# Turning the gated rows of routed tiles through memory instead of on TensorE in a one-core mLSTM and mixture-of-experts kernel

## The chip, the cores and the metric

The kernel runs on one core of one Trainium2 chip. The time is device microseconds of one execution. Of the kernel before the change three executions were timed.

## The reference, cut to what matters

The input x has 8 x 512 = 4096 tokens of 1024 floats. The first half of the layer adds a gated mLSTM cross attention; the change does not touch it. The second half normalises the rows and adds a mixture of experts:

```
probs = softmax(flat @ router_w.T); topk_w, topk_idx = top_k(probs, 2)     # 16 experts, 2 for each token
shared = (silu(flat @ shared_gate_w) * (flat @ shared_up_w)) @ shared_down_w   # inner width 1024
xs = flat[sorted_tok]                                   # rows sorted by expert
g = ragged_dot(xs, gate_w, group_sizes); u = ragged_dot(xs, up_w, group_sizes) # inner width 512
dn = ragged_dot(silu(g) * u, down_w, group_sizes)
out = x + tanh(g_ffn) * (shared + scatter_add(sorted_w * dn))
```

Everything is float32. The product silu(g) * u, a tile of 128 tokens by 512, is what this text calls the gated rows, h. For the third matrix product h must stand with its 512 columns on the partitions, so each tile of h has to be turned.

## The kernel before, in words

The kernel has two blocks. The first, `mix_block`, does the attention, the routing and half of the shared expert. The second, `ffn_block`, runs the 16 routed experts over tiles of 128 gathered tokens (at least two tiles for an expert, 73 tiles in all) and after them the other half of the shared expert over 32 tiles. The change is in `ffn_block` alone. Each matrix product is made of three in a faster format: a high part of the one factor by a high part of the other, and the two mixed products with the low parts. So a tile takes 48 matmuls for gate and up (line 1608, into `p_g` and `p_up`) and 24 for down (line 1594, into `p_y`), and every operand, weights too, is split into a high part by ScalarE (a copy) and a low part by VectorE (a subtraction).

No planner sets the order. Each engine has a program of its own (`@block.sync`, `@block.gpsimd`, and so on), in which `tiles` (line 1172 and on) calls that engine's `body` once for each tile i; semaphores tie them together. PE is one tile ahead of itself: in the body of tile i it makes gate and up of tile i and then `down`, which is the third product of tile i-1. The turn of h of tile i-1 has to be done by then.

- Routed tiles before: `turn_h` of PE (line 1581) makes four transposes of 128x128 into the PSUM tile `p_h`, in the middle of gate and up of the next tile; ScalarE copies the high part out (`h_high`, line 1377), VectorE subtracts for the low part (`h_low`, line 1462), and `down` waits for that.
- Shared tiles, before and after: `h_store` (line 1366) sends h, 256 KB, from ScalarE's DMA queue to the memory tensor `mid_h`, in rows of 512 B. `h_quarters` (line 1372) waits until that has landed and fetches it back into h with four rows on one partition, 2 KB for each partition. VectorE's `turn_h` (line 1457) then turns squares of 32x32, ScalarE's `turned_high` (line 1383) takes the high part and `h_low` the low one.

ScalarE's body runs in this order: the weight split `split_gu` if the tile is its expert's first (8 pieces, line 1354), the right half of y out of PSUM (`y_right`, line 1406), the high part of the turned h, then a wait for gate and up, tanh (line 1422), the high part of the next x tile (`x_high`, line 1394), the left half of y (`y_left`, line 1401), and in a first tile `split_d` (4 pieces, line 1361). VectorE's body: low parts of the weights (line 1439) in a first tile, then h, then the turn of the next tile's x (`turn_x`, line 1473), then the two multiplications that make h (`silu_up`, lines 1485 and 1490), then the low part of x (`x_low`, line 1479), then in a first tile the low parts of the down weights.

SP's queue carries the weights (`load_weights`, line 1120) and the stores of y (`store_routed`, line 1223). The three weight tensors of an expert are 2 MB each; gate and up arrive in rows of 2 KB, down in rows of 16 KB. SP asks for those of expert e+1 after the last y store of expert e-1, when expert e's own are split, so in the second tile of expert e. GpSimd gathers the x rows of each routed tile (lines 1290 to 1300) through the third queue. In the page, q1 is SP's queue, q10 ScalarE's and q0 GpSimd's.

Of the kernel before, what the change touches and what calls it, by code (L numbers as in the profile page):

```python
# [15 lines left out]
NE, FE, FS = 16, 512, 1024  # L16
# [13 lines left out]
GUP = 8  # L30
# [1092 lines left out]
def ffn_block(nc, t, keep):  # L1123
# [4 lines left out]
    with ExitStack() as ctx:  # L1128
# [60 lines left out]
            body(n + (NCH - 1), n + (NCH - 2), NE, NCH - 1, False, "shared", True)  # L1189
            finish(n + NCH, n + (NCH - 1), NE, NCH)  # L1190

        def start(eng, e, less=0):

            return eng.value_load(starts_i[0:1, less, bass.ds(e, 1)], min_val=MIN_TILES - less, max_val=MAX_TILES - less)

        xn_quarters = t["xn"].rearrange("(c j t) (a d) -> c a j t d", t=4, j=32, a=4)
        xn_flat = t["xn"].rearrange("c (a d) -> (c a) d", a=4)
# [12 lines left out]

        @block.sync
        def _(sp):
            def load_weights(e):

                ge(sp, gu_split, GUP * e)
                weights_in(sp, stage, expert_weights(t, e, 1), slice(0, 2), (wg_in, wu_in))
                ge(sp, d_split, (PIECES - GUP) * e)
                weights_in(sp, stage, expert_weights(t, e, 1), slice(2, 3), (wd_in,))

            def store_routed(q):  # L1220

                sp.wait_ge(y_rdy, 2 * q + 2)
                sp.dma_start(t["y"][bass.ds(q * P, P), :], y[:, :]).then_inc(y_out, 16)

            def load_base(c):
                ge(sp, z_rdy, c)
                sp.dma_start(base_row[:, :], base_rows[c]).then_inc(base_in, 16)

            def store_joined(c):

                sp.wait_ge(z_rdy, c)
                sp.dma_start(z_rows[c - 1], y[:, :]).then_inc(z_out, 16)

            load_weights(1)

            store_routed(0)
            with sp.Fori(2, start(sp, 1)) as i:
                store_routed(i - 1)
            with sp.Fori(1, NE - 1) as e:
                store_routed(start(sp, e, 1))  # L1240
                load_weights(e + 1)
                with sp.Fori(start(sp, e) + 1, start(sp, e + 1)) as i:
                    store_routed(i - 1)
            store_routed(start(sp, NE - 1, 1))
            load_weights(NE)
            with sp.Fori(start(sp, NE - 1) + 1, start(sp, NE)) as i:
                store_routed(i - 1)
            store_routed(start(sp, NE, 1))
            before = start(sp, NE)

            def load_x(c):
                sp.wait_ge(x_turned, before + c)
                quarters_in(sp, c, xs_in)

            for n in range(2):
                sp.wait_ge(mid_out[n], 16 * NCH // 2)
            load_base(0)
            load_x(2)
            with sp.Fori(1, NCH - 4) as c:
                load_x(c + 2)  # L1260
                load_base(c)
                store_joined(c)
            for left in (4, 3, 2, 1):
                c = NCH - left
                if left > 2:
                    load_x(c + 2)
                if left > 1:
                    load_base(c)
                else:
                    ge(sp, gu_split, GUP * (NE + 1))  # L1270
                    sp.dma_start(last_base, base_rows[c]).then_inc(last_base_in, 16)
                store_joined(c)
            for n in range(2):
                half = slice(512 * n, 512 * n + 512)
                sp.wait_ge(last_z, n + 1)
                sp.dma_start(z_rows[NCH - 1][:, half], y[:, half]).then_inc(z_out, 16)
            sp.wait_ge(z_out, 16 * (NCH + 1))
# [67 lines left out]

        @block.scalar
        def _(act):
            def split_gu(i, e):

                act.wait_ge(wg_in, 16 * e + 16)  # L1350
                act.wait_ge(wu_in, 16 * e + 16)
                ge(act, gu_ps, i)
                for p in range(GUP):
                    nc.scalar.activation(w_hi[:, p, :], stage[:, p, :], ACT.Copy).then_inc(gu_hi, 1)

            def split_d(i, e, prev):
                act.wait_ge(wd_in, 16 * e + 16)
                if prev:
                    act.wait_ge(y_ps, 2 * i)
                for p in range(GUP, PIECES):  # L1360
                    nc.scalar.activation(w_hi[:, p, :], stage[:, p, :], ACT.Copy).then_inc(d_hi, 1)  # L1361

            def h_store(c):

                act.wait_ge(h_rdy, start(act, NE) + (c + 1))
                act.dma_start(t["h"].rearrange("a s f -> s a f"), h[:, :].rearrange("p (a f) -> p a f", a=4)
                              ).then_inc(hs_out, 16)

            def h_quarters(c):

                act.wait_ge(hs_out, 16 * c)
                act.dma_start(h[:, :], t["h"].rearrange("a (j t) f -> (a j) (t f)", t=4)).then_inc(hq_in, 16)

            def h_high(i):

                act.wait_ge(ht_ps, i)
                nc.scalar.activation(ht_hi[:, :, :], p_h[:, :, :], ACT.Copy).then_inc(ht_hi_rdy, 1)  # L1377

            def turned_high(c, q):

                act.wait_ge(y_ps, 2 * q)
                act.wait_ge(h_turned, c)
                nc.scalar.activation(ht_hi[:, :, :], h_t[:, :, :], ACT.Copy).then_inc(ht_hi_rdy, 1)

            def last_high(c):

                act.wait_ge(ht_ps, start(act, NE) + 1)
                nc.scalar.activation(ht_hi[:, :, :], p_h[:, :, :], ACT.Copy).then_inc(ht_hi_rdy, 1)

            def x_high(i):  # L1390

                act.wait_ge(x_turned, i + 1)
                for n in range(2):
                    nc.scalar.activation(xt_hi[:, 4 * n:4 * n + 4, :], x_t[:, 4 * n:4 * n + 4, :],  # L1394
                                         ACT.Copy).then_inc(xt_hi_rdy, 1)

            def y_left(q):

                ge(act, y_out, 16 * q)
                act.wait_ge(y_ps, 2 * q + 1)  # L1400
                nc.scalar.activation(y[:, 0:512], p_y[0][:, :], ACT.Copy).then_inc(y_rdy, 1)

            def y_right(q):

                act.wait_ge(y_ps, 2 * q)
                nc.scalar.activation(y[:, 512:D], p_y[1][:, :], ACT.Copy).then_inc(y_rdy, 1)

            def body(i, q, e, c, first, prev, last):
                if first and not (isinstance(i, int) and i == 0):
                    split_gu(i, e)  # L1410
                if callable(q):
                    q = q()

                if not (isinstance(i, int) and i < 2) and (c is None or isinstance(c, int) and c < 2):
                    y_right(q)
                if prev == "shared":
                    h_quarters(c)
                    turned_high(c, q)
                elif prev:
                    h_high(i)  # L1420
                act.wait_ge(gu_ps, i + 1)
                nc.scalar.activation(th[:, :], p_g[:, :], ACT.Tanh, scale=0.5).then_inc(tanh_rdy, 1)  # L1422
                if not last:
                    x_high(i + 1)
                    if c is not None:
                        h_store(c)
                if prev == "routed":
                    y_left(q)
                if first:
                    split_d(i, e, prev)  # L1430

            x_high(0)
            tiles(act, body, lambda i, q, e, c: last_high(c))

        @block.vector
        def _(dve):
# [13 lines left out]
                for p in range(GUP, PIECES):  # L1450
                    split(p, d_hi, (PIECES - GUP) * e + (p - GUP + 1), d_split)

            def turn_h(i, c):

                dve.wait_ge(xt_rdy, 2 * i)
                dve.wait_ge(hq_in, 16 * c)
                nc.vector.transpose(h_t[:, :, :].rearrange("p k (j t) -> p t k j", t=4),
                                    h[:, :].rearrange("p (t i k) -> p t k i", t=4, k=FE // P)).then_inc(h_turned, 1)

# [22 lines left out]
            def silu_up(i, c):  # L1482
# [2 lines left out]
                nc.vector.scalar_tensor_tensor(out=th[:, :], in0=th[:, :], scalar=1.0, in1=p_g[:, :],  # L1485
                                               op0=ALU.add, op1=ALU.mult).then_inc(silu_step, 1)
                dve.wait_ge(silu_step, i + 1)
                if c is not None:
                    ge(dve, h_turned, c)
                nc.vector.scalar_tensor_tensor(out=h[:, :], in0=th[:, :], scalar=0.5, in1=p_up[:, :],  # L1490
                                               op0=ALU.mult, op1=ALU.mult).then_inc(h_rdy, 1)

# [52 lines left out]
            def body(i, q, e, c, first, prev, last):  # L1545
                if first:
                    split_gu(i, e)
                if prev == "shared":
                    turn_h(i, c)
                    h_low(i, h_t)  # L1550
                elif prev:
                    h_low(i, p_h)
                if not last:
                    turn_x(i + 1, c)
                silu_up(i, c)
# [18 lines left out]
        def _(pe):  # L1574
# [23 lines left out]
            def body(i, q, e, c, first, prev, last):  # L1598
                ge(pe, h_rdy, i)
                for k in range(KD):  # L1600
# [3 lines left out]
                    for m, (a, w) in enumerate(trio):  # L1604
                        if m == 2:
                            pe.wait_ge(gu_split, GUP * e + (k + 1))
                        for out, o in ((p_g, 0), (p_up, FE)):
                            mm = nc.tensor.matmul(out[:, :], a[:, k, :], w[:, k, o:o + FE],  # L1608
                                                  start=(k == 0 and m == 0), stop=(k == KD - 1 and m == 2))
                    if k == 3 and prev == "routed":  # L1610
                        turn_h(i)
                mm.then_inc(gu_ps, 1)
                if prev:
                    down(i, e - 1 if first else e)
# [71 lines left out]
```

## Time and profile before

| what | value |
|---|---|
| median of three runs | 2929.71 us (2923.65 to 2931.17) |
| profiled execution, span | 2941.0 us |
| PE busy in it | 2784.3 us (95%) |
| VectorE busy | 1845.4 us (63%) |
| ScalarE busy | 1015.8 us (35%) |
| DMA, mean | 156 GB/s, 458.24 MB |
| routed tiles | about 1185 to 2421 us |
| shared tiles | about 2421 to 2941 us |

The profile comes from one execution. For it the page gives the span, from the first to the last instruction, and no other time of its own; the span is 11.3 us (0.4%) above the median of the timed runs. A matmul's busy time of about 0.39 us overlaps that of its neighbours, so the pace is read from the starts of successive groups, not from busy times. Times in the rows are microseconds from the span's start.

### The profile page before, as it was taken

The numbers are of one execution on the slowest core, as the hardware profiler recorded it, in microseconds if no ns is written. First come the engines' busy times: TensorE is split into PE (matmuls) and PEld (weight loads), VectorE is DVE, ScalarE is ACT, GpSimd is POOL, SyncE is SP. The second block draws the span as 40 slices with busy tenths as digits, with TensorE's granted clock in tenths as the row PEclk, the third lists the DMA queues.
The fourth block names the chain that finished last, engine by engine and source line by source line (L and its number), as shares of the span: only waits on it lengthen the run. The fifth ranks groups of instructions, "written<-read, shape, count | busy, mean of one in ns | idle before, by whom it ended". The sixth has DMA issues, their size and how long they took to land.

```text
span 2941.0 us, 49274 instructions
## 1 busy us (share of the span) xinstructions
PE 2784.3 (95%) x17322; PEld 2290.3 (78%) x17323; DVE 1845.4 (63%) x2800; ACT 1015.8 (35%) x1948; POOL 996.6 (34%) x1148
## 2 busy tenths in 40 slices
PE   3799999999999986999999999999999999999999
PEld 2677777777777774788888888888888888888887
DVE  3787878878887854454555545545545546767676
ACT  4445444444444421233333333333333331111111
POOL 1334433434344423343343443443443411111111
PEclk7799999999999997999999999999999999999999
DMA  6445545554555541344444444443443327666665
GB/s 196 148 158 170 159 141 162 166 153 152 162 169 159 145 166 65 136 150 150 145 150 148 146 153 144 146 153 143 148 152 143 100 108 213 182 203 183 203 182 182
DMA packets 243470, 458.24 MB, mean 156 GB/s; under 512 B 99696, under 2 KB 131824, under 8 KB 240624
## 3 DMA queue, kind: packets, MB, share of 16 engines
q1 hardware_dynamic: 116976, 333.62, 33.9%
q0 software_dynamic: 34880, 73.10, 8.1%
q10 hardware_dynamic: 91488, 49.82, 6.3%
q8 instruction: 81, 1.33, 0.2%
q14 instruction: 45, 0.37, 0.0%
HBM read 358.96 MB, written 115.31 MB: 161 GB/s over the span
## 4 chain that ended last, share of the span: by engine, by line
PE 59%; DVE 1%; issue 0%; ACT 0%; DMA 0%; SPq 0%; ACTq 0%; DVEq 0%
PE p_g_b L1608 19%; PE p_up_b L1608 19%; PE p_y_b L1594 19%; PE p_h_b L1581 1%; DVE x_t_b L1473 0%; DVE w_lo L1439 0%; DMA xn<-mid_xn 0%; ACT w_hi L1361 0%; SPq L1204 0%; DVE xt_lo_b L1479 0%; ACT xt_hi_b L1394 0%; DVE th_b L1485 0%; DVE x L1515 0%; DVE x L1506 0%; DVE y_b L1517 0%
## 5 line engine op out<-in xcount | busy, mean ns | idle before, releaser
L1300 POOL DMA_INDIRECT xn<-mid_xn,idx_q x284 | 304.5, 1072 | 512.6 <-DVE x_t_b L1473 424.6
L1608 PE MATMUL p_g_b<-w_hi,xt_hi_b 128*128 128x512 f32 x840 | 334.6, 398 | 19.8 <-DVE xt_lo_b L1479 16.9
L1594 PE MATMUL p_y_b<-w_hi,ht_hi_b 128*128 128x512 f32 x840 | 327.4, 390 | 1.9 <-DVE ht_lo_b L1462 1.9
L1608 PE MATMUL p_g_b<-w_lo,xt_hi_b 128*128 128x512 f32 x840 | 328.6, 391 | 0.0
L1608 PE MATMUL p_g_b<-w_hi,xt_lo_b 128*128 128x512 f32 x840 | 328.4, 391 | 0.0
L1608 PE MATMUL p_up_b<-w_hi,xt_lo_b 128*128 128x512 f32 x840 | 328.0, 390 | 0.0
L1608 PE MATMUL p_up_b<-w_hi,xt_hi_b 128*128 128x512 f32 x840 | 327.8, 390 | 0.0
L1608 PE MATMUL p_up_b<-w_lo,xt_hi_b 128*128 128x512 f32 x840 | 327.7, 390 | 0.0
L1594 PE MATMUL p_y_b<-w_hi,ht_lo_b 128*128 128x512 f32 x840 | 327.5, 390 | 0.0
L1594 PE MATMUL p_y_b<-w_lo,ht_hi_b 128*128 128x512 f32 x840 | 327.4, 390 | 0.0
L1462 DVE TENSOR_TENSOR ht_lo_b<-p_h_b,ht_hi_b 128x512 fp32r<-128x512 f32 x74 | 51.0, 690 | 367.5 <-ACT ht_hi_b L1377 367.5
L1439 DVE TENSOR_TENSOR w_lo<-stage,w_hi 128x1024 fp32r<-128x1024 f32 x200 | 230.2, 1219 | 79.8 <-ACT w_hi L1361 49.2
L1422 ACT ACTIVATE th_b<-p_g_b 128x512 f32<-128x512 f32 x105 | 62.8, 598 | 547.0 <-PE p_up_b L1608 543.6
L1485 DVE SCALAR_TENSOR_TENSOR th_b<-th_b,p_g_b 128x512 f32<-128x512 f32 x105 | 72.2, 688 | 281.0 <-ACT th_b L1422 271.9
L1473 DVE STREAM_TRANSPOSE x_t_b<-xn 128x1024 f32<-128x1024 f32 x104 | 235.0, 2259 | 16.6 <-PEq L76 12.6
L1006 PE MATMUL p_g<-w_hi,xt 128*128 128x512 f32 x512 | 212.8, 416 | 0.0
L1006 PE MATMUL p_up<-w_hi,xt 128*128 128x512 f32 x512 | 202.3, 395 | 0.0
L1608 PEld LDWEIGHTS p_g_b<-w_hi,xt_hi_b 128*128 128x128 f32 x840 | 158.9, 189 | 50.9 <-DVE xt_lo_b L1479 17.9
L1608 PEld LDWEIGHTS p_g_b<-w_lo,xt_hi_b 128*128 128x128 f32 x840 | 157.9, 188 | 38.9 <-DVE w_lo L1439 5.6
L1594 PEld LDWEIGHTS p_y_b<-w_hi,ht_hi_b 128*128 128x128 f32 x840 | 158.1, 188 | 34.9 <-DVE ht_lo_b L1462 2.1
L591 ACT ACTIVATE stage<-stage,cols 128x128 f32<-128x128 f32 x512 | 153.8, 389 | 90.4 <-POOL stage L456 90.3
L1608 PEld LDWEIGHTS p_g_b<-w_hi,xt_lo_b 128*128 128x128 f32 x840 | 157.9, 188 | 33.8
(224 smaller groups left out, 5585.8 us busy)
## 6 DMA issues: line engine op xcount, KB each, us to landing
mid_y<-y_b SPq DMA_DIRECT2D x73, 512.0 KB, 2.6
stage<-mid_g_row SPq DMA_DIRECT2D x64, 512.0 KB, 5.4
stage<-in_eg SPq DMA_DIRECT2D x16, 2048.0 KB
stage<-in_eu SPq DMA_DIRECT2D x16, 2048.0 KB
stage<-in_ed SPq DMA_DIRECT2D x16, 2048.0 KB
mid_y<-in_x SPq DMA_DIRECT2D x34, 512.0 KB
stage<-in_x SPq DMA_DIRECT2D x32, 512.0 KB
stage<-in_ctx_t ACTq DMA_DIRECT2D x32, 512.0 KB, 8.9
```

The costliest lines, as they stand in the source:

```text
L591: nc.scalar.activation(gbd[:, h, :], gbd[:, h, :], ACT.Exp, bias=cols[:, j, 0, h:h + 1]).then_inc(d_rdy, 1)
L1006: last = nc.tensor.matmul(out[:, :], xt[:, a, k, :], w[:, k, o:o + FE], start=(k == 0 and m == 0), stop=(k == KD - 1 and m == 2))
L1300: nc.gpsimd.indirect_dma_start(out=xg_parts[:, n, :], out_offset=None, in_=xn_flat, in_offset=bass.IndirectOffsetOnAxis(ap=idx_q[:, n:n + ...
L1422: nc.scalar.activation(th[:, :], p_g[:, :], ACT.Tanh, scale=0.5).then_inc(tanh_rdy, 1)
L1439: nc.vector.tensor_tensor(w_lo[:, p, :], stage[:, p, :], w_hi[:, p, :].bitcast(f32), ALU.subtract).then_inc(sem_lo, 1)
L1462: nc.vector.tensor_tensor(ht_lo[:, :, :], source[:, :, :], ht_hi[:, :, :].bitcast(f32), ALU.subtract).then_inc(ht_rdy, 1)
L1473: nc.vector.transpose(x_t[:, :, :].rearrange("p k (j t) -> p t k j", t=4), parts.rearrange("p t (i k) -> p t k i", k=KD)).then_inc(x_turne ...
L1485: nc.vector.scalar_tensor_tensor(out=th[:, :], in0=th[:, :], scalar=1.0, in1=p_g[:, :], op0=ALU.add, op1=ALU.mult).then_inc(silu_step, 1)
L1581: last = nc.tensor.transpose(p_h[:, k, :], h[:, k:FE:FE // P], ident[:, :])
L1594: last = nc.tensor.matmul(p_y[n][:, :], a[:, k, :], b[:, GUP + k, w], start=(k == 0 and m == 0), stop=(k == FE // P - 1 and m == 2))
L1608: mm = nc.tensor.matmul(out[:, :], a[:, k, :], w[:, k, o:o + FE], start=(k == 0 and m == 0), stop=(k == KD - 1 and m == 2))
```

## The change

Routed tiles take the way of the shared ones: PE's transposes go, and h of every tile is stored, fetched back and turned on VectorE. In an expert's first tile the fetch is issued in the middle of `split_gu`. `h_store` follows `x_high`; `silu_up` now waits in every tile until the turn of the tile before is done. PE's `turn_h` stays for the last tile alone, in `finish`. SP's `load_weights` is cut in two functions that are called one behind the other, and the loop of y stores is written out by one turn.

```diff
         def _(sp):
-            def load_weights(e):
+            def load_gate_up(e):
                 ge(sp, gu_split, GUP * e)
                 weights_in(sp, stage, expert_weights(t, e, 1), slice(0, 2), (wg_in, wu_in))
+            def load_down(e):
                 ge(sp, d_split, (PIECES - GUP) * e)
                 weights_in(sp, stage, expert_weights(t, e, 1), slice(2, 3), (wd_in,))
...
+            def store_expert(e, after):
+                store_routed(start(sp, e, 1))
+                load_gate_up(after)
+                load_down(after)
+                store_routed(start(sp, e, 0, MIN_TILES))
+                with sp.Fori(start(sp, e) + 2, start(sp, e + 1)) as i:
+                    store_routed(i - 1)
...
             with sp.Fori(1, NE - 1) as e:
-                store_routed(start(sp, e, 1))
-                load_weights(e + 1)
-                with sp.Fori(start(sp, e) + 1, start(sp, e + 1)) as i:
-                    store_routed(i - 1)
+                store_expert(e, e + 1)
...
         def _(act):
-            def split_gu(i, e):
+            def split_gu(i, e, prev):
...
                 for p in range(GUP):
+                    if p == GUP // 2 and prev:
+                        h_quarters(i)
                     nc.scalar.activation(w_hi[:, p, :], stage[:, p, :], ACT.Copy).then_inc(gu_hi, 1)
...
-                if prev == "shared":
-                    h_quarters(c)
-                    turned_high(c, q)
-                elif prev:
-                    h_high(i)
+                if prev:
+                    if not first:
+                        h_quarters(i)
+                    turned_high(i, q)
                 act.wait_ge(gu_ps, i + 1)
                 nc.scalar.activation(th[:, :], p_g[:, :], ACT.Tanh, scale=0.5).then_inc(tanh_rdy, 1)
                 if not last:
                     x_high(i + 1)
-                    if c is not None:
-                        h_store(c)
+                    h_store(i)
...
         def _(dve):
-                if prev == "shared":
-                    turn_h(i, c)
+                if prev:
+                    turn_h(i)
                     h_low(i, h_t)
-                elif prev:
-                    h_low(i, p_h)
...
-                if c is not None:
-                    ge(dve, h_turned, c)
+                ge(dve, h_turned, i)
...
         def _(pe):
-                    if k == 3 and prev == "routed":
-                        turn_h(i)
```

## Rows read from the trace of the kernel before

**Rows 1.** Page, busy time: us, share of the span, instructions.
```profile
PE 2784.3 (95%) x17322; PEld 2290.3 (78%) x17323; DVE 1845.4 (63%) x2800; ACT 1015.8 (35%) x1948; POOL 996.6 (34%) x1148
```
**Rows 2.** Page, DMA issues: count, KB each, median us to landing.
```profile
mid_y<-y_b SPq DMA_DIRECT2D x73, 512.0 KB, 2.6
stage<-in_eg SPq DMA_DIRECT2D x16, 2048.0 KB
```
**Rows 3.** Chain of waits, routed (1536 to 1571) and shared tiles: start, us, what.
```profile
1536.66 5.44 PE p_y_b L1594 x24
1547.54 0.47 PE p_h_b L1581 x4
1553.51 5.44 PE p_y_b L1594 x24
...
1570.59 5.44 PE p_y_b L1594 x24
...
2448.59 5.44 PE p_y_b L1594 x24
...
2464.91 5.44 PE p_y_b L1594 x24
```
**Rows 4.** Timeline, ScalarE and VectorE in one shared tile: start, us, engine, line.
```profile
2499.65 0.38 ACTq L1366 DMA_DIRECT2D mid_h<-h_b  x1
2502.68 0.33 ACTq L1372 DMA_DIRECT2D h_b<-mid_h  x1
...
2505.97 1.10 DVE L1457 STREAM_TRANSPOSE h_t_b<-h_b 128x512 f32<-128x512 f32 x1
...
2507.83 0.69 DVE L1462 TENSOR_TENSOR ht_lo_b<-h_t_b,ht_hi_b 128x512 fp32r<-128x512 f32 x1 [0.76 <-ACT ht_hi_b L1383]
```
**Rows 5.** One line's instructions, the fetch of h in shared tiles: time to landing.
```profile
DMA to landing us min/median/max: 2.6/2.6/2.7
```
**Rows 6.** Timeline, ScalarE and VectorE, first and second tile of one expert.
```profile
1557.42 7.70 ACT L1354 ACTIVATE w_hi<-stage 128x1024 fp32r<-128x1024 f32 x8 [0.56 <-issue]
...
1579.88 0.57 ACT L1406 ACTIVATE y_b<-p_y_b 128x512 f32<-128x512 f32 x1
...
1558.51 9.17 DVE L1439 TENSOR_TENSOR w_lo<-stage,w_hi 128x1024 fp32r<-128x1024 f32 x8 [1.72 <-ACT w_hi L1354]
...
1583.22 2.29 DVE L1473 STREAM_TRANSPOSE x_t_b<-xn 128x1024 f32<-128x1024 f32 x1
...
1588.82 0.69 DVE L1490 SCALAR_TENSOR_TENSOR h_b<-th_b,p_up_b 128x512 f32<-128x512 f32 x1
```
**Rows 7.** Timeline, SP's queue, same expert.
```profile
1582.77 3.23 SPq L1120 DMA_DIRECT2D stage<-in_ed  x1
1593.69 0.35 SPq L1223 DMA_DIRECT2D mid_y<-y_b  x1
```
**Rows 8.** DMA queues, 1585 to 1586: packets, MB, share of 16 engines.
```profile
q1 hardware_dynamic: 202, 0.41, 106.4%
```
**Rows 9.** DMA queues, 1598 to 1599.
```profile
q1 hardware_dynamic: 24, 0.39, 92.8%
q0 software_dynamic: 24, 0.00, 1.4%
```
**Rows 10.** One line's instructions, y store of 1593.69: time to landing.
```profile
DMA to landing us min/median/max: 9.1/9.1/9.1
```
**Rows 11.** One line's instructions, index loads of 1591.5 to 1593.1: time to landing.
```profile
DMA to landing us min/median/max: 5.8/6.9/8.0
```
**Rows 12.** Timeline, ScalarE's queue: a load in the first block, beside SP's transfers.
```profile
645.11 0.33 ACTq L548 DMA_DIRECT2D stage<-in_ctx_t  x1
```
**Rows 13.** DMA queues, 648 to 649 (none of q10 before it).
```profile
q10 hardware_dynamic: 16, 0.07, 28.2%
```
**Rows 14.** Windows: us, busy of PE, PEld, DVE, ACT, POOL; PEclk, DMA share, GB/s.
```profile
1085.00:1086.00 1.00, 0.00 (x0) 0.00 (x0) 0.76 (x2) 0.35 (x1) 0.77 (x1) 1.00 0.04 7
1088.00:1089.00 1.00, 1.00 (x4) 0.81 (x3) 0.96 (x2) 0.00 (x0) 0.00 (x0) 0.50 0.00 0
1090.00:1091.00 1.00, 1.00 (x5) 0.85 (x4) 0.38 (x2) 0.00 (x0) 0.29 (x2) 0.89 0.00 0
1186.00:1187.00 1.00, 0.00 (x0) 0.00 (x0) 1.00 (x2) 1.00 (x3) 0.36 (x1) 1.00 1.03 371
```

More of the change, by code:

```diff
@@ L1190, in tiles, with start @@
             finish(n + NCH, n + (NCH - 1), NE, NCH)
-        def start(eng, e, less=0):
-            return eng.value_load(starts_i[0:1, less, bass.ds(e, 1)], min_val=MIN_TILES - less, max_val=MAX_TILES - less)
+        def start(eng, e, less=0, left=0):
+            return eng.value_load(starts_i[0:1, less, bass.ds(e, 1)], min_val=MIN_TILES - less,
+                                  max_val=MAX_TILES - left - less)
         xn_quarters = t["xn"].rearrange("(c j t) (a d) -> c a j t d", t=4, j=32, a=4)
@@ L1232, in store_joined @@
                 sp.dma_start(z_rows[c - 1], y[:, :]).then_inc(z_out, 16)
-            load_weights(1)
+            def store_expert(e, after):
[5 more added lines that the diff above has]
+                    store_routed(i - 1)
+            load_gate_up(1)
+            load_down(1)
             store_routed(0)
@@ L1239, in _ @@
             with sp.Fori(1, NE - 1) as e:
-                store_routed(start(sp, e, 1))
-                load_weights(e + 1)
-                with sp.Fori(start(sp, e) + 1, start(sp, e + 1)) as i:
-                    store_routed(i - 1)
[L1244 to L1247, printed above, removed]
+                store_expert(e, e + 1)
+            store_expert(NE - 1, NE)
             store_routed(start(sp, NE, 1))
@@ L1361, in split_d, with h_store, h_quarters, turned_high @@
                     nc.scalar.activation(w_hi[:, p, :], stage[:, p, :], ACT.Copy).then_inc(d_hi, 1)
-            def h_store(c):
-                act.wait_ge(h_rdy, start(act, NE) + (c + 1))
+            def h_store(i):
+                act.wait_ge(h_rdy, i + 1)
                 act.dma_start(t["h"].rearrange("a s f -> s a f"), h[:, :].rearrange("p (a f) -> p a f", a=4)
                               ).then_inc(hs_out, 16)
-            def h_quarters(c):
-                act.wait_ge(hs_out, 16 * c)
+            def h_quarters(i):
+                act.wait_ge(hs_out, 16 * i)
                 act.dma_start(h[:, :], t["h"].rearrange("a (j t) f -> (a j) (t f)", t=4)).then_inc(hq_in, 16)
[L1374 to L1382, printed above, removed]
+            def turned_high(i, q):
+                ge(act, y_ps, 2 * q)
+                act.wait_ge(h_turned, i)
                 nc.scalar.activation(ht_hi[:, :, :], h_t[:, :, :], ACT.Copy).then_inc(ht_hi_rdy, 1)
             def last_high(c):
-                act.wait_ge(ht_ps, start(act, NE) + 1)
+                act.wait_ge(ht_ps, 1)
                 nc.scalar.activation(ht_hi[:, :, :], p_h[:, :, :], ACT.Copy).then_inc(ht_hi_rdy, 1)
@@ L1409, in body @@
                 if first and not (isinstance(i, int) and i == 0):
-                    split_gu(i, e)
+                    split_gu(i, e, prev)
                 if callable(q):
@@ L1451, in split_d, with turn_h @@
                     split(p, d_hi, (PIECES - GUP) * e + (p - GUP + 1), d_split)
-            def turn_h(i, c):
-                dve.wait_ge(xt_rdy, 2 * i)
-                dve.wait_ge(hq_in, 16 * c)
+            def turn_h(i):
+                dve.wait_ge(hq_in, 16 * i)
                 nc.vector.transpose(h_t[:, :, :].rearrange("p k (j t) -> p t k j", t=4),
```

## Prediction

> **What bounds the kernel now.** I read the page's busy times first: PE is busy for 95% of the span [rows 1], so a microsecond taken off PE is a microsecond off the kernel if whatever feeds PE keeps up. Second, the chain of waits over the routed tiles: it runs through PE's matmuls alone, and the start of one down group to the next is the pace. A tile that isn't its expert's first takes 1553.51 - 1536.66 = 16.85 us, a first tile 1570.59 - 1553.51 = 17.08, a shared tile 2464.91 - 2448.59 = 16.32 [rows 3]. The shared tile has the same 72 matmuls and no transposes, and turns h by way of memory. Third, timelines of the engines that feed PE, to see how late each result may come; fourth, bytes by DMA queue, since the new way of h depends on transfers that must get through beside others.
>
> **What is removed.** PE's four transposes, 0.47 us on the chain [rows 3], and a little around them: 16.85 - 16.32 = 0.53 us a tile. There are 73 routed tiles [rows 2], and each is turned inside the next tile's body; the turn in `finish` stays. 73 x 0.53 = **-38.7 us**. Bounds: the 0.47 of the transposes alone gives -34, the 0.53 is the top.
>
> **What is added, in a tile without weight traffic.** ScalarE issues a store and a fetch (0.38 and 0.33 us), VectorE turns h (1.10). From the store's issue to the fetch's is 2502.68 - 2499.65 = 3.03 us, the store's landing [rows 4]; the fetch lands after 2.6 [rows 5]; from the start of the turn to the end of the low part is 2507.83 + 0.69 - 2505.97 = 2.55 [rows 4], say 2.65 with PE's start. In the routed body the fetch goes out after `y_right`, 6.1 us after PE's down begins (5.44 [rows 3] and a copy of 0.6), when the store, sent at about 2.5, has landed. 6.1 + 2.6 + 2.65 = 11.4, against 16.32 when PE needs it: 4.9 us to spare, and the round trip is hidden behind gate and up. If transfers take longer by more than 4.9 us together, PE waits for the rest. Cost 0, bounds 0 and 0, for the shared tiles run at this pace.
>
> **The first tile of an expert** (16 of them, the shared expert's first among them). VectorE splits eight weight pieces until 1558.51 + 9.17 = 1567.68 [rows 6], and the turn of h comes behind them: 1567.68 + 2.65 = 1570.33. PE, rid of the transposes, would be ready at 1570.59 - 0.53 = 1570.06 [rows 3]. It waits 0.3 us: **+5 us**. The fetch in the middle of ScalarE's split costs 0.33 there, and VectorE's pieces (9.17/8 = 1.15 us) are slower than ScalarE's (7.70/8 = 0.96), so the lag is absorbed. Behind VectorE's turn wait the turn of the next x and `silu_up`; both have PE's 5.44 us of down as cover. Bounds 0 and 0.6, so 0 and +10.
>
> **The second tile** (15, those in which the next expert's weights are asked for: 16 loads of a gate tensor [rows 2], less the two of experts 0 and 1, asked for earlier, and the shared half's). On the clock of before, less what the first tile gained (0.2): the fetch goes out at 1580.3, behind `y_right` [rows 6], lands at 1582.9, h is turned and split at 1585.6, and PE needs it at 1570.36 + 16.32 = 1586.7. The weights' descriptors go out at the same time (the down tensor's at 1582.77 [rows 7]), so I take 0.2 us a tile: **+3 us**, bounds 0 and +15 (a fetch 2 us late).
>
> **The third tile** decides. VectorE's turn of x, 2.29 us [rows 6], now ends at about 1585.6 + 2.3 = 1587.9; `silu_up` follows (two times 0.69), so this h is stored at about 1589.4, in the midst of 6 MB of weights on SP's queue, which run at 0.4 MB/us [rows 8] from about 1582.7. Against gate and up packets of 2 KB (16/202 = 0.08 us each [rows 8]) it goes quickly, but those end near 1595; some 25 of the 32 may be through. A packet of down weights takes 16/24 = 0.65 us, and there are eight for each engine, until 1600; with gathers, the store and the y store in between, I put the store's landing at 1602. Below, its landing is 1589.4 + 3.0 = 1592.4 [rows 4]. Above, it is that of the y store that stands behind all weights, 1593.69 + 9.1 = 1602.8 [rows 7, 10]. Nearest are the four index loads: issued at 1591.5 to 1593.1 on a third queue, they landed 5.8 to 8.0 us later, so near 1599 [rows 11], with far fewer packets for each engine. Only then does ScalarE, which stands at that wait, issue the fetch: 1602.1 + 2.6 + 2.65 = 1607.3. PE needs it at 1586.9 + 16.32 = 1603.2. PE waits **4.2 us x 15 = +63 us**. From the lower end the fetch waits for `y_right` at 1593.1 and h is there at 1598.4: no wait. From the upper end it is 4.9, and 5.5 with a fetch slowed by the y store: so 0 and +83. Queued behind ScalarE's wait are its high part, tanh and next x; behind VectorE's the next turn of x and `silu_up`. They restart together, 2.3 + 1.4 + 0.7 us after the low part, inside PE's 5.44 us of down, so the wait is paid once.
>
> The Trainium skill, page "DMA: Bandwidth & Descriptors", section "Queues, rings and completion order", has an engine drain a whole packet of about 9 to 17 descriptors before it changes queues; equal counts of 24 [rows 9] speak for one at a time. What the page's dozen would make of the store is the second rival below.
>
> **The clock.** In the first block PE once stood idle for most of four microseconds, the window of 1085 among them; the granted clock then fell to 0.50, the lower of its two levels (1.2 of 2.4 GHz), as at 1088, and was back at the upper one within the window of 1090 [rows 14]: about 3.4 us at half speed, which costs 1.7. After a shorter idle, 2.8 us around 1186, it stayed at 1.00 [rows 14]. A wait of 4.2 us lies above both, so I count 1.2 us (1.7 in about seven of ten): **+18 us**, bounds 0 and +45 (3 us each).
>
> **SP's edit: 0.** Before, too, gate, up and down are asked for one behind the other, after the same three waits (last y store, gate and up split, down split), and the y stores follow in the same order; the down tensor's issue 1.5 us behind the gate's shows it [rows 7]. What is new there is register work in an engine that waits. Bounds 0 and 0: the change as named does nothing here.
>
> **Sum.** -38.7 + 5 + 3 + 63 + 18 = +50 us. It is made on the profiled execution, whose span is 2941.0 us, 0.4% above the median of the runs; I add it to the median: 2929.7 + 50.3 = **2980 us**.
>
> **Rivals.** (1) The round trip is hidden in every tile: the store gets its share while gate and up weights move, the third tile waits for nothing. Then -38.7 + 5 + 3 = -31, 2899 us. For it: every shared tile does so, with 4.9 us to spare, and if the store starts at once (1590) its 32 turns of 0.15 us end before the down weights begin. Against it: the late starts [rows 12, 13] and landings [rows 10, 11] under load. It decides from a landing of the store at about 1597.8: earlier than that, no wait. (2) An engine serves a dozen packets of one queue at a turn. The store needs three turns, beside gate and up, and lands near 1596.5; the fetch then waits for one turn of eight down packets, 5.2 us, lands near 1601.3, and PE waits 0.8 us: -31 + 12 = -19, 2911 us. (3) Store early, fetch late by single turns: the store lands at 1599 and the fetch with the last weights, near 1602.5; PE waits 2 us and the clock stays: -31 + 30 = -1, 2929 us. (4) Each wait reaches 5.5 us and costs 3 us of clock: -31 + 83 + 45 = +97, 3027 us.
>
> **Chances.** Forecast 0.56, with its own range 2945 to 3010; rival 1 0.16; rival 2 0.08; rival 3 0.10, divided between the three outcomes (0.02 faster, 0.06 same, 0.02 slower); rival 4 0.10. I give faster 0.26, same 0.06, slower 0.68; 0.3%, 9 us, is about what a measurement of this kernel can tell from no change. Range 2895 to 3030.
>
> **What would show it.** Right: no `p_h` transposes but the last four, 16.32 us between down groups without weight traffic, and in each expert's third tile PE waiting some 4 us for `ht_lo` with the store of h landing 10 us or more after its issue; a granted clock of 0.50 behind many of these waits. Wrong: h stores that land within 8 us beside the weights; a wait in other tiles, which would mean that the 4.9 us are not there; or a wait for x tiles, whose gathers the later turn of x also moves back.

## The result, and the profile after

The changed kernel takes 3013.3 us (median of four runs, 3009.2 to 3019.5); the kernel before, run beside it on the same chip, 2929.1. The ratio is 1.0293, with a 95% interval of 1.0277 to 1.0309: 84 us slower, where +50 was forecast (2980 us, range 2895 to 3030). The sign and the place of the loss were as forecast, its size was not.

The page of the changed kernel: its span, the busy times that answer to [rows 1], PE's line of waits from the fifth part, and DMA issues as in [rows 2] (with the median time to landing).

```profile
span 3017.9 us, 49030 instructions
...
PE 2791.0 (92%) x17030; PEld 2273.6 (75%) x17031; DVE 1921.9 (64%) x2873; ACT 1022.1 (34%) x1948; POOL 981.7 (33%) x1148
...
L1592 PE MATMUL p_y_b<-w_hi,ht_hi_b 128*128 128x512 f32 x840 | 344.8, 410 | 78.0 <-DVE ht_lo_b L1463 78.0
...
stage<-in_ed SPq DMA_DIRECT2D x16, 2048.0 KB, 19.4
mid_h<-h_b ACTq DMA_DIRECT2D x104, 256.0 KB, 2.7
h_b<-mid_h ACTq DMA_DIRECT2D x104, 256.0 KB, 2.7
```

PE issues 292 instructions fewer, the 73 times four transposes, and still is busy 6.7 us longer: matmuls at the lower clock last longer (its windows are shown further down). It is 92% busy instead of 95%, and 78.0 us of idle time now stand ahead of `down`, put down to the low part of the turned h. The median store and fetch of h land in 2.7 us: a median over 104 does not show the trouble, which is in fifteen of them.

The pace by place in the expert, from the starts of successive down groups (means over the experts, 72 periods in all):

| tile of the expert | count | before | after | PE's idle time ahead of `down`, after |
|---|---|---|---|---|
| first | 16 | 17.07 | 17.47 | 0.22 |
| second | 15 | 16.85 | 16.45 | 0 |
| third | 15 | 16.85 | 21.29 | 4.81 |
| fourth | 15 | 16.85 | 18.44 | 0 |
| fifth | 8 | 16.85 | 16.32 | 0 |
| sum of 72 (3 more lie ahead of expert 1) | | 1216.6 | 1301.9 | |

The sums differ by 85.3 us, as much as the median changed. (The spans of the two profiled executions differ by 76.9 us only, 3017.9 - 2941.0, since the first down group of the profiled execution of before began at 1198.7 us and that of after at 1190.5.) One third tile on the chain of waits (start, us, what); the matmuls of gate and up that end at 1601 and those after 1631 are left out:

```profile
1584.50 5.73 PE p_y_b L1592 x24
...
1601.15 0.61 ACT th_b L1425
1601.78 0.70 DVE th_b L1486
1602.50 0.70 DVE h_b L1490
1603.22 12.43 DMA mid_h<-h_b
1615.66 4.44 DMA h_b<-mid_h
1620.13 1.11 DVE h_t_b L1458
1621.32 0.64 ACT ht_hi_b L1387
1621.98 0.70 DVE ht_lo_b L1463
1622.80 8.33 PE p_y_b L1592 x24
```

Where the chain of before ran through PE alone [rows 3], it now leaves PE for 21.7 us: h is made, stored in 12.43 us and fetched in 4.44. The 24 matmuls behind take 8.33 us instead of 5.44 [rows 3]. SP's queue in the same stretch answers to [rows 7], and the store that stands behind the weights to [rows 10]:

```profile
1595.45 0.58 SPq L1120 DMA_DIRECT2D stage<-in_eg  x1
...
1596.98 5.37 SPq L1120 DMA_DIRECT2D stage<-in_ed  x1
1607.37 0.35 SPq L1227 DMA_DIRECT2D mid_y<-y_b  x1
```

```profile
DMA to landing us min/median/max: 12.2/12.2/12.2
```

What the DMA engines did in between, by queue, as in [rows 8, 9]: packets, MB, share of 16 engines. First the microsecond from 1608, gate and up on q1; then the one from 1613, the down weights on q1:

```profile
q1 hardware_dynamic: 122, 0.25, 64.5%
q10 hardware_dynamic: 126, 0.06, 21.3%
q0 software_dynamic: 27, 0.09, 21.2%
...
q1 hardware_dynamic: 27, 0.44, 103.2%
q10 hardware_dynamic: 18, 0.01, 2.8%
q0 software_dynamic: 21, 0.00, 1.2%
```

Beside packets of 2 KB the store (q10) gets 126 of its 512 packets through in a microsecond; beside packets of 16 KB it gets 18, with nearly all of the engines' time gone to the weights. Of the store's 32 packets for each engine some 27 pass from 1607 to 1611 and the last five take four microseconds more.

### The profile page after: what moved, and what is told of

The parts are those of the page before. It is cut to its first block, busy times and chain, and to the rows that moved or that the text cites. A ratio compares the mean times of both kernels' runs of the same rounds, so it can differ in the third digit from the quotient of the medians.

```text
span 3017.9 us, 49030 instructions
## 1 busy us (share of the span) xinstructions
PE 2791.0 (92%) x17030; PEld 2273.6 (75%) x17031; DVE 1921.9 (64%) x2873; ACT 1022.1 (34%) x1948; POOL 981.7 (33%) x1148
## 3 DMA queue, kind: packets, MB, share of 16 engines
q1 hardware_dynamic: 116976, 333.62, 32.6%
## 4 chain that ended last, share of the span: by engine, by line
PE 41%; DMA 10%; DVE 5%; ACT 4%; issue 2%; ACTq 0%; POOL 0%; DVEq 0%; POOLq 0%
PE p_y_b L1592 15%; PE p_g_b L1606 13%; PE p_up_b L1606 13%; DMA mid_h<-h_b 8%; ACT w_hi L1363 3%; DMA h_b<-mid_h 2%; DVE w_lo L1441 1%; DVE h_t_b L1458 1%; DVE ht_lo_b L1463 1%; DVE th_b L1486 1%; DVE h_b L1490 1%; ACT ht_hi_b L1387 1%; ACT th_b L1425 1%; ACTq L1194 0%; DMA xn<-mid_xn,idx_q 0%
## 5 line engine op out<-in xcount | busy, mean ns | idle before, releaser
L1307 POOL DMA_INDIRECT xn<-mid_xn,idx_q x284 | 297.3, 1047 | 562.5 <-DVE x_t_b L1474 472.0
L1592 PE MATMUL p_y_b<-w_hi,ht_hi_b 128*128 128x512 f32 x840 | 344.8, 410 | 78.0 <-DVE ht_lo_b L1463 78.0
L1458 DVE STREAM_TRANSPOSE h_t_b<-h_b 128x512 f32<-128x512 f32 x104 | 115.4, 1110 | 379.4 <-DMA h_b<-mid_h 378.4
L1592 PE MATMUL p_y_b<-w_hi,ht_lo_b 128*128 128x512 f32 x840 | 338.9, 404 | 0.0
L1592 PE MATMUL p_y_b<-w_lo,ht_hi_b 128*128 128x512 f32 x840 | 338.0, 402 | 0.0
L1387 ACT ACTIVATE ht_hi_b<-h_t_b 128x512 fp32r<-128x512 f32 x104 | 65.7, 632 | 639.9 <-DVE h_t_b L1458 639.9
L1592 PEld LDWEIGHTS p_y_b<-w_hi,ht_hi_b 128*128 128x128 f32 x840 | 165.5, 197 | 126.0 <-issue 88.1
L1474 DVE STREAM_TRANSPOSE x_t_b<-xn 128x1024 f32<-128x1024 f32 x104 | 231.6, 2227 | 18.7 <-PEq L76 12.1
L1592 PEld LDWEIGHTS p_y_b<-w_lo,ht_hi_b 128*128 128x128 f32 x840 | 165.1, 197 | 36.3
L1592 PEld LDWEIGHTS p_y_b<-w_hi,ht_lo_b 128*128 128x128 f32 x840 | 166.0, 198 | 34.3
## 6 DMA issues: line engine op xcount, KB each, us to landing
stage<-in_ed SPq DMA_DIRECT2D x16, 2048.0 KB, 19.4
```

What stands on the lines that cost most here:

```text
L1307: nc.gpsimd.indirect_dma_start(out=xg_parts[:, n, :], out_offset=None, in_=xn_flat, in_offset=bass.IndirectOffsetOnAxis(ap=idx_q[:, n:n + ...
L1474: nc.vector.transpose(x_t[:, :, :].rearrange("p k (j t) -> p t k j", t=4), parts.rearrange("p t (i k) -> p t k i", k=KD)).then_inc(x_turne ...
L1592: last = nc.tensor.matmul(p_y[n][:, :], a[:, k, :], b[:, GUP + k, w], start=(k == 0 and m == 0), stop=(k == FE // P - 1 and m == 2))
```

## The experiments

All ratios are to the kernel before, run beside each on the same chip (2926.4 us for the first four, 2927.8 for the last four). The edits are cut to the lines that matter, with `...` for what is left out.

**The order on SP's queue by itself.** The kernel before with SP's part of the change alone.

```diff
+            def store_expert(e, after):
+                store_routed(start(sp, e, 1))
+                load_gate_up(after)
+                load_down(after)
...
```

> The kernel before with SP's edit alone (load_weights cut in two, y stores written out by one turn); h of routed tiles is still turned on TensorE. My theory: the three weight tensors were asked for one behind the other before too, after the same waits, so nothing moves: 2929 us, ratio 1.000 within 0.003. Rival: the written-out stores or the requests cost something of their own, then up to the whole +84 us, 3013.

Measured: 2925.9 us, ratio 1.0004 (0.9992 to 1.0017). SP's edit does nothing; the whole loss is the new way of h.

**Smaller packets for the down weights.** The changed kernel, every weight tensor in column blocks of 512, so that the down weights too move in packets of 2 KB instead of 16 KB.

```diff
-        eng.dma_start(place, matrix.rearrange("(p k) f -> p k f", p=P)).then_inc(sem, 16)
+        for lo in range(0, matrix.shape[1], FE):
+            eng.dma_start(place[:, :, lo:lo + FE], matrix[:, lo:lo + FE].rearrange("(p k) f -> p k f", p=P)).then_inc(sem, 16)
```

> The kernel after, with the down weights fetched in two halves of 512 columns, so in packets of 2 KB instead of 16 KB; the bytes, their order and the moment of the request stay. Theory (turns): queues take turns packet by packet, so the 32 packets of an h store for each engine get through beside 2 KB packets; the store of the third tile lands 8 to 9 us after its issue instead of 12.4 to 14, PE waits about 2 us there instead of 4.9, mostly without a fall of the clock: 15 x (2.9 + 2.1) = 75 us less than 3013, about 2940. Rival (bytes): the store lands when 6 MB ahead of it have drained, whatever the packets: no change, 3013.

Measured: 2989.8 us, ratio 1.0219 (1.0200 to 1.0238). The third tile's store lands 8.7 to 9.4 us after its issue instead of 12.4 to 14.0, so packet size sets the store's landing. But the fetch, issued earlier, now meets the rest of the down weights and takes 5.7 to 6.5 us instead of 2.5 to 4.4; PE's wait falls only from 4.81 to 3.77 us and the clock still falls behind all fifteen waits. About 2940 us was expected; that was wrong because it priced the fetch as in a free queue. The rival by bytes, a store that lands when the 6 MB have drained, is out. One store and one fetch on its chain:

```profile
1587.81 8.76 DMA mid_h<-h_b
1596.59 6.01 DMA h_b<-mid_h
```

**The down weights requested later, in two steps.** First behind the y store that follows, then behind the third tile's fetch of h.

```diff
             def store_expert(e, after):
                 store_routed(start(sp, e, 1))
                 load_gate_up(after)
-                load_down(after)
                 store_routed(start(sp, e, 0, MIN_TILES))
+                load_down(after)
```

> The kernel after, with the down weights asked for one y store later (gate and up, y store of the first tile, down), some 11 us later than now. Theory (turns): the h store of the third tile then meets gate and up packets alone and lands after 9 us, but its fetch meets the 16 KB packets of down and lands some 5.5 us after its issue; PE's wait in the third tile falls from 4.9 to about 3.3 us and some falls of the clock go: about 2980 us. Rival (bytes): the same bytes are asked for in the same stretch, the fetch takes the place of the store as the late one: 3013. Second rival: down weights that come later make the next expert wait: slower than 3013.

Measured: 2991.2 us, ratio 1.0216 (1.0198 to 1.0234). The store lands after 7.8 to 9.9 us, the fetch after 6.2 to 7.7: it, in its turn, stands beside the 16 KB packets. PE waits 4.02 us, where 3.3 was expected with a fetch of 5.5 us. The loss moved from one transfer to the other. The next expert does not wait for its later down weights: first tiles take 17.49 us, against 17.47.

```diff
-            def load_down(e):
+            def load_down(e, fetched=0):
                 ge(sp, d_split, (PIECES - GUP) * e)
+                ge(sp, hq_in, 16 * fetched)
...
-                load_down(after)
                 store_routed(start(sp, e, 0, MIN_TILES))
+                load_down(after, start(sp, e, 0, MIN_TILES) + 2)
```

> The kernel after, with the down weights asked for only when h of the expert's second tile has been stored and fetched back (a wait of SP on that fetch ahead of the request). Theory (turns): neither transfer of that h meets a 16 KB packet; the store lands after 9 us, the fetch after 2.6, PE waits 0.3 to 0.5 us in the third tile and the clock stays up: 15 x (4.5 + 2.1) = 99 us less, about 2914, which is 0.5% faster than before. Rival (VectorE's order): what PE waits for is VectorE, which turns h ahead of its other work; its program is the same here, so 3013 stays. Rival (bytes): gate and up alone still hold the store up until they have drained, which is at about 9 us, so near 2914 as well.

Measured: 2907.4 us, ratio 0.9935 (0.9918 to 0.9951): faster than both kernels. The store lands after 7.4 to 9.5 us, beside gate and up alone, the fetch after 2.5 to 2.8; third tiles take 16.48 us, fourth tiles 16.37, and the granted clock is 1.00 all through its routed tiles. VectorE's program is that of the changed kernel, so its order was not what PE waited for. The 72 periods sum to 1198.9 us, 17.7 less than before. Timelines of SP and ScalarE around one third tile (store of h at 1569.01):

```profile
1561.24 0.58 SPq L1120 DMA_DIRECT2D stage<-in_eg  x1
...
1573.16 0.36 SPq L1228 DMA_DIRECT2D mid_y<-y_b  x1
1579.92 0.36 SPq L1120 DMA_DIRECT2D stage<-in_ed  x1
```

```profile
1569.01 0.38 ACTq L1376 DMA_DIRECT2D mid_h<-h_b  x1
...
1577.30 0.33 ACTq L1382 DMA_DIRECT2D h_b<-mid_h  x1
```

The down weights are asked for at 1579.92, when the fetch has landed, and the median one lands in 7.5 us instead of 19.4. PE's waits over all routed tiles (us in total, times, longest), first of the changed kernel, then of this one:

```profile
PE p_y_b L1592 <- DVE ht_lo_b L1463: 76.1, 32, 6.7
```

```profile
PE p_y_b L1593 <- DVE ht_lo_b L1464: 5.3, 20, 0.7
```

**Packets counted, not bytes.** The changed kernel with h stored in rows of 2 KB and fetched in pieces of 512 B, the same bytes both ways.

```diff
-                act.dma_start(t["h"].rearrange("a s f -> s a f"), h[:, :].rearrange("p (a f) -> p a f", a=4)
-                              ).then_inc(hs_out, 16)
+                act.dma_start(t["h"], h[:, :]).then_inc(hs_out, 16)
...
-                act.dma_start(h[:, :], t["h"].rearrange("a (j t) f -> (a j) (t f)", t=4)).then_inc(hq_in, 16)
+                for a in range(4):
+                    act.dma_start(h[32 * a:32 * a + 32, :].rearrange("p (t f) -> p t f", t=4),
+                                  t["h"][:, P * a:P * a + P].rearrange("(j t) f -> j t f", t=4)).then_inc(hq_in, 16)
```

> The changed kernel with the same 256 KB of h written in 128 packets of 2 KB (8 for each of 16 engines) instead of 512 of 512 B (32 for each), and fetched back in 512 packets of 512 B by four requests; the down weights stay in packets of 16 KB. If an engine gives the queues one packet in turn, the count decides: 8 turns, nearly all beside the 2 KB packets of gate and up, so the third tile's store lands 5 to 8 us after its issue instead of 12.4 to 14.0; the fetch then goes out near 1610 and has 32 turns beside what is left of the 16 KB packets, so it takes 6 to 9 us instead of 2.5 to 4.4, and PE waits 2 to 4 us in place of 4.8: 2955 to 3000 us. Rival, the queues share the engines by bytes: the store has the same bytes and still lands 12 us or more after its issue, and the time stays at 3013 or grows by the slower fetch.

Measured: the stores of third tiles land after 6.0 to 6.9 us (one after 8.1), the first of the fetch's four parts after 6.2 to 8.4, and the whole fetch, from the first issue to the last landing, takes 7.1 to 10.5: the store as the turns say, the fetch a little longer than the 6 to 9 expected, and the rival by bytes is out. The DMA queues in two microseconds of it: from 1606, store beside gate and up, all of 2 KB; and from 1613, the 512 B pieces of the fetch beside down weights:

```profile
q1 hardware_dynamic: 73, 0.15, 39.1%
q10 hardware_dynamic: 68, 0.14, 36.4%
q0 software_dynamic: 39, 0.09, 25.2%
...
q1 hardware_dynamic: 24, 0.39, 94.5%
q10 hardware_dynamic: 21, 0.01, 3.6%
q0 software_dynamic: 14, 0.00, 0.8%
```

Near equal counts both times, 73 to 68 and 24 to 21, at sizes of 1:1 and 32:1. The time I had expected, 2955 to 3000 us, was missed: 3015.8, ratio 1.0301 (1.0286 to 1.0316). PE's wait in third tiles is 4.32 us, 0.3 above what I had given, partly because the four requests alone take 2.52 us of ScalarE's queue. In the trace its 72 periods are 10 us shorter than the changed kernel's (1291.8); but its profiled execution was the fastest of its four (3008.2 us) and that of the changed kernel the slowest (3019.5), and the timed runs do not confirm a gain.

**What the first tile still loses.** Three kernels. In the first, the left half of y is copied out ahead of the right half, in the next body, so that ScalarE can begin the split of the weights earlier; the second makes the same edit in the kernel before; the third moves the fetch of h behind the split:

```diff
             def body(i, q, e, c, first, prev, last):
...
+                    y_left(q)
                     y_right(q)
...
-                if prev == "routed":
-                    y_left(q)
```

> The version with the down weights requested behind the third tile's fetch (2907 us), and in it the left half of y copied out ahead of the right half, in the next tile's body, instead of at the end of its own. In a first tile ScalarE then starts the split of the gate and up weights some 2 us after PE's down begins and not 4.5 us after. Theory: what the first tile has over an ordinary one (17.49 against 16.32 us) is ScalarE's late split, since PE waits for a high part, a low part and the turned h: first tiles near 16.4, 16 x 1.1 = 17 us less, 2890 us. Rival: VectorE's chain of pieces is the bound: no change, 2907.

> The kernel before with that same later copy of the left half of y alone, as a control. Its first tile takes 17.07 against 16.85 us, so at most 16 x 0.22 = 3.5 us are to be had: 2923 to 2927. A loss would say that the copy costs where it now stands.

> The version with the down weights requested behind the third tile's fetch (2907 us), and in it the first tile's fetch of h issued after the whole split of ScalarE instead of in its middle. Theory: the fetch takes 0.33 us of ScalarE there and nothing more, and after the split it lands some 0.6 us after VectorE is done with its pieces, so first tiles take about 0.5 us longer, 16 x 0.5 = +8: 2915 us. Rival: the fetch in mid-split is what makes the high parts late: first tiles near 17.0, 2900 us.

Measured: on the version with the late down weights 2911.0 us, ratio 0.9938 (0.9925 to 0.9950), so no gain over 0.9935; first tiles 17.09 instead of 17.49 us, about a third of what was expected, and what they gain is lost again in one third tile of 21.03 us, whose h was stored some 4 us later than in the others (VectorE's turn of the next x had waited 5.2 us for gathered rows), and in fourth tiles of 16.46. On the kernel before 2924.6 us, ratio 0.9986 (0.9977 to 0.9995), as expected: its first tiles take 16.85 us like the others. With the fetch behind the split 2911.8 us, ratio 0.9942 (0.9929 to 0.9955), first tiles 17.46: neither the loss nor the gain. The place of that fetch is free: it goes out 5.7 us behind the start of the down group instead of some 5.0, and lands long before VectorE is done with its pieces.

What PE's weight loads waited for in routed tiles (us, times, longest), in the version with the late down weights, and then with the late copy of y as well:

```profile
PEld p_g_b L1607 <- ACT w_hi L1364: 8.4, 15, 0.6
PEld p_g_b L1607 <- DVE w_lo L1442: 7.9, 16, 0.5
```

```profile
PEld p_g_b L1607 <- DVE w_lo L1442: 7.2, 15, 0.5
...
PEld p_g_b L1607 <- ACT w_hi L1365: 1.9, 9, 0.4
```

The earlier split takes away most of the wait for the high part, but VectorE's low part stays late, and so does the turn behind it. Theory and rival each had a share of it.

## Why the prediction was right and wrong

The mechanism was the forecast's: the third tile's store of h is caught among the next expert's weights, ScalarE stands at its landing, PE waits, and the clock falls. The version with the late down weights shows it by taking the 16 KB packets out of the round trip's way: the wait and the fall of the clock are gone, some 105 us less than the changed kernel (1.0293 - 0.9935 of 2928). The steps, with what each measured (per tile, times the count; the periods of after against those of before):

| step | forecast | measured |
|---|---|---|
| transposes gone | 0.53 x 73 = -38.7 | 16.85 to 16.32 in fifth tiles: 0.53 |
| first tile waits | 0.3 x 16 = +5 | 17.47 - (17.08 - 0.53) = 0.92: +14.7 |
| second tile | 0.2 x 15 = +3 | 0.13: +2 |
| third tile waits | 4.2 x 15 = +63 | 21.29 - 16.32 = 4.97: +74.6 |
| clock | 1.2 x 15 = +18 | 18.44 - 16.32 = 2.12: +31.8 |
| SP's edit | 0 | ratio 1.0004 |
| sum | +50 | +84 |

Three terms were mis-sized, by 10, 12 and 14 us; they all erred the same way.

**The third tile.** The store was to go out 18.8 us after the down group's start and did at 18.7 (1603.22 - 1584.50). That agreement is luck, for it came by another path. The forecast had VectorE's turn of the next x last, ending at 17.3 (1587.9 - 1570.59), because it let the second tile's fetch go out at 9.7 (1580.3 - 1570.59); that fetch went out at 6.6 and the turn of x ended at 16.1. What `silu_up` waited for was the tanh behind PE's last matmul of gate and up:

```profile
1598.38 2.23 DVE L1474 STREAM_TRANSPOSE x_t_b<-xn 128x1024 f32<-128x1024 f32 x1
1601.78 0.69 DVE L1486 SCALAR_TENSOR_TENSOR th_b<-th_b,p_g_b 128x512 f32<-128x512 f32 x1 [1.16 <-ACT th_b L1425]
```

In one expert of the fifteen VectorE did come last, since its turn of x waited 2.90 us for gathered rows: the store went out at 20.4 and the third tile took 23.19 us, the longest. That is the wait for x tiles which the forecast named as a sign of being wrong, in one tile only:

```profile
1749.04 2.23 DVE L1474 STREAM_TRANSPOSE x_t_b<-xn 128x1024 f32<-128x1024 f32 x1 [2.90 <-DMA xn<-mid_xn,idx_q]
```

The store was to land 12.6 us after its issue and landed 13.3 later on average over the fifteen; the fetch took 2.8 on average instead of 2.6, 4.4 in the tile shown, where the store came through earlier and the fetch met the last down packets. That is 0.9 of late h. PE itself would have been ready 0.2 later than assumed (16.45 + 16.32 = 32.8 after the second tile's down group, against 1603.2 - 1570.59 = 32.6), which leaves 4.9, near the 4.97 measured. (The idle time of 4.81 counts from the end of the matmul before, whose busy time of 0.39 us overlaps the next one's by 0.16.) The late start came as read from [rows 12, 13], and later: the store's first packets moved 3.7 us after the issue (none before 1606.9), where the forecast had 3.1. The step that failed in size is the landing: I let the down weights end at 29.4 us after the down group's start; in the fourteen tiles with an expert's weights they landed 31.7 to 33.7 after it, with the store's and the gathers' turns between them (0.22 to 0.27 MB of weights in a microsecond from 1606 to 1610, against 0.41 in [rows 8]).

**The clock.** I took 1.7 us in seven of ten. It fell behind all fifteen waits (the shortest fourth tile takes 17.77 us, 1.45 over 16.32), and in eight of them it stayed down longer than in [rows 14]. Windows of the changed kernel, columns as there:

```profile
1618.00:1619.00 1.00, 0.00 (x0) 0.00 (x0) 0.00 (x0) 0.00 (x0) 0.00 (x0) 1.00 0.25 100
...
1621.00:1622.00 1.00, 0.00 (x0) 0.00 (x0) 0.24 (x2) 0.68 (x2) 0.00 (x0) 0.77 0.00 0
1622.00:1623.00 1.00, 0.20 (x1) 0.20 (x2) 1.00 (x2) 0.43 (x1) 0.00 (x0) 0.50 0.00 0
...
1627.00:1628.00 1.00, 1.00 (x4) 0.80 (x3) 0.16 (x1) 0.00 (x0) 1.00 (x1) 0.50 1.00 273
1628.00:1629.00 1.00, 1.00 (x5) 0.80 (x4) 0.00 (x0) 0.60 (x1) 0.70 (x2) 0.82 0.58 172
```

PE restarts at 1622.80 and is back at the upper level (2.4 GHz) within the window of 1628: some 5.5 us of matmuls at the lower one (1.2 GHz), where I had counted 3.4. Half of 5.5 is the 2.7 us that this fourth tile took over 16.32 (1641.85 - 1622.80 = 19.05). The failed step is to have sized the fall by one case of the first block, and to have counted seven falls in ten where all fifteen came.

**The first tile.** I put VectorE's eight pieces where they were before, 5.00 us behind the start of down (1558.51 - 1553.51, [rows 3, 6]). But 1553.51 on the chain is where the matmul ahead of that group ends; the first matmul of the group starts 0.16 earlier:

```profile
1553.35 0.39 PE L1594 MATMUL p_y_b<-w_hi,ht_hi_b 128*128 128x512 f32 x1
```

From there the pieces start 5.16 us later, and the forecast's own wait of 0.27 (1570.33 - 1570.06) becomes 0.43. In the changed kernel they start 5.63 behind the first matmul, at 1572.72, with down at 1567.09:

```profile
1567.09 0.39 PE L1592 MATMUL p_y_b<-w_hi,ht_hi_b 128*128 128x512 f32 x1
```

```profile
1569.36 0.38 ACTq L1375 DMA_DIRECT2D mid_h<-h_b  x1
1570.01 0.60 ACT L1405 ACTIVATE y_b<-p_y_b 128x512 f32<-128x512 f32 x1 [1.08 <-PE p_y_b L1592]
1571.63 1.06 ACT L1363 ACTIVATE w_hi<-stage 128x1024 fp32r<-128x1024 f32 x1 [1.01 <-issue]
```

```profile
1572.72 9.17 DVE L1441 TENSOR_TENSOR w_lo<-stage,w_hi 128x1024 fp32r<-128x1024 f32 x8 [2.18 <-ACT w_hi L1363]
```

The 0.47 by which the pieces start later (5.63 - 5.16) and the 0.43 make 0.90, nearly the measured excess of 0.92. ScalarE stood at 1.01 us of issue ahead of its first piece, 0.56 before [rows 6]. The step that failed is to have left the pieces where they were: "the lag is absorbed" looked at the fetch among the pieces, which costs nothing, as the version with the fetch behind the split shows, and not at what now stands ahead of them. More than half of that extra 0.45 us is a longer load of a register on ScalarE's queue, 0.53 us against 0.28 before; why it is longer is not settled.

**The rivals.** Rival 1, every round trip hidden, 2899 us, is out for the kernel as changed. The version with the late down weights comes to it, 2907, and the point from which it was to decide held: a landing 27.2 us behind the down group's start (1597.8 - 1570.59). In that version the ten landings up to 27.4 us behind it cost PE nothing (27.0 in the tile shown, 1577.30 - 1550.28), and the five from 27.5 to 28.2 cost 0.1 to 0.8 us. Rival 2, a dozen packets of one queue at a turn, is out: it had the store land within some 7 us of its issue (1596.5 - 1589.4), where it took 12.4 to 14.0 us, and the last five of its 32 packets for each engine came through over four microseconds and not in one turn. The Trainium skill's page "DMA: Bandwidth & Descriptors", section "Queues, rings and completion order", has an engine drain some 9 to 17 descriptors of one queue before it switches; the trace does not agree, if a packet of the profile is one of the page's descriptors. Rival 3, an early store and a late fetch, is what smaller down packets (2990 us) and the request behind the y store (2991) produced: it then costs nearly as much, not 2 us of waiting. Rival 4, 3027 us, lies nearer to the measured time than the forecast does, in part by luck: its sizes, 5.5 us of wait and 3 of clock, were too large (4.97 and 2.12), and the 10 us of the first tile, which it lacked as well, make up for part of that.

## What to carry to other kernels

A transfer that is short when alone is priced by the number of its packets and by the size of the packets beside it: here some 0.15 us for each packet of an engine beside packets of 2 KB (27 in four microseconds), 0.8 beside packets of 16 KB (the last five in four more). Before a round trip through memory is put on a path that PE waits for, look for the largest packets in flight at that time, and request those behind the round trip rather than ahead of it; moving only one half of the trip out of the way moves the loss to the other. A stall of four to five microseconds of PE cost here two fifths as much again in clock (2.12 on 4.97).

## What the runs showed of the hardware

- Two busy queues share by count of packets and not by bytes: 73 to 68 in a microsecond at 2 KB each, 24 to 21 at 16 KB against 512 B. Where the turns are taken, in the engines or where packets are made, no run here shows.
- The first packet of a ScalarE store beside SP's weights moves 3.7 us after the issue (1603.22, none before 1606.9), and in the first block that of a load moved at least 2.9 us after its issue [rows 12, 13]; without weights beside it a store's first packet moves 0.9 to 1.6 us after. Why is open.
- PE's waits of 4.3 us and more were followed by a fall of the clock and a slower fourth tile in all fifteen cases of the changed kernel, and so were those of 3.2 us and more in the version with the request behind the y store; in the late-copy version the clock did not fall behind a wait of 2.9 us, and the tile behind it took at most 16.47 us.
- ScalarE's queue runs ahead of its activations: the fetch in the first tile was issued at 1572.03, while the first piece of the split (1571.63, 1.06 us) was still running, and that in the second tile at 1591.14, ahead of the `y_right` that stands before it in the program (1594.08).
